# Attention and experts on one core: the second norm's transposes and the router logits in a fourth stage, a new table of places, and a reordered start

## The reference

```python
x = x + _layernorm(attn(_layernorm(x)))         # 16 heads of 8, causal, relative positions clipped to +-2
x = x + _layernorm(ffn(_layernorm(x)))

# attn: Q, K, V = x @ W + b per head
scores = (Q K^T + Q . rel_k[idx]) / sqrt(8);  causal mask;  softmax
out    = (attn V + attn . rel_v[idx]) @ W_o + b_o
# ffn
shared = (silu(x @ sw1) * (x @ sw3)) @ sw2
s      = sigmoid(x @ router_w.T);  top 2 of s + router_bias;  gates = s_sel / sum
routed = sum over the two experts e of gate_e * (gelu(x @ ew1[e]) @ ew2[e])
```

## Time and profile before

| | us |
|---|---|
| median of 3 runs (1090.37 to 1091.61) | 1090.96 |
| the profiled execution | 1092.7 |
| its span, first to last instruction | 1090.6 |
| start, to the first score matmul | 48.7 |
| steps 1 to 17 | 724.2 (48.7 to 772.9) |
| rest of the first phase | 32.3 (to 805.2) |
| second phase | 285.4 |

### The profile page before, as it was taken

How to read it: one execution, slowest core, us unless ns; L and a number is a source line. 1 busy time by engine, 2 the same in 40 slices (tenths; PEclk the granted TensorE clock), 3 DMA queues, 4 the chain that set the end, 5 groups by cost and what they waited for, 6 DMA issues and landing times. The chain is left out here.

```text
span 1090.6 us, 25410 instructions
## 1 busy us (share of the span) xinstructions
PE 945.4 (87%) x8551; PEld 557.6 (51%) x8551; DVE 854.2 (78%) x2060; ACT 693.6 (64%) x1309; POOL 725.9 (67%) x935
## 2 busy tenths in 40 slices
PE   0378999999999999999999999996658999999995
PEld 0144455455454454554554544542246777777774
DVE  4187888888888888888888888887158888888884
ACT  3424776776776767767766768665235766676763
POOL 2133666768658668677586686665355988988986
PEclk9988999999999999999999999998669999999999
DMA  5100101101001001010010010102313545455551
GB/s 141 56 23 27 35 22 36 38 20 44 31 21 50 21 32 42 20 41 33 20 49 21 32 46 20 38 12 54 115 48 118 160 149 163 154 164 156 158 156 31
DMA packets 61452, 70.87 MB, mean 65 GB/s; under 512 B 9504, under 2 KB 39072, under 8 KB 61344
## 3 DMA queue, kind: packets, MB, share of 16 engines
q1 hardware_dynamic: 61344, 69.47, 20.4%
HBM read 43.75 MB, written 8.65 MB: 48 GB/s over the span
## 5 line engine op out<-in xcount | busy, mean ns | idle before, releaser
L1071 DVE TENSOR_REDUCE mx<-ps_s 128x1 f32<-128x512 f32 (+2 forms) x640 | 412.1, 683 | 94.6 <-PE ps_s L1458 89.9
L759 ACT ACTIVATE prob<-ps_e 128x512 f32<-128x512 f32 x640 | 348.6, 601 | 131.0 <-PE ps_e L1424 131.0
L614 POOL TENSOR_SCALAR_AFFINE_SELECT prob<-prob 128x516 f32<-128x516 f32 (+1 forms) x320 | 172.8, 564 | 187.4 <-ACT prob L759 187.4
L1447 PE MATMUL ps_s<-ks,qs 63*128 63x512 f16 (+3 forms) x1024 | 230.3, 308 | 36.8 <-DMA ks<-kl 17.0
L713 POOL TENSOR_TENSOR hidden_low<-hidden,hidden_high 128x512 fp32r<-128x512 f32 x144 | 190.4, 1350 | 21.5 <-ACT hidden_high L949 20.2
L1424 PE MATMUL ps_e<-qs,ks 64*128 64x512 f16 (+3 forms) x1024 | 185.3, 303 | 9.1 <-DMA qs<-mT 4.4
L1475 PE MATMUL ps_av<-prob,vp 128*32 128x512 f32 (+3 forms) x2048 | 181.5, 450 | 9.3 <-POOL prob L614 9.3
L1458 PE MATMUL ps_s<-maskb,identb 64*128 64x129 bf16 (+1 forms) x1024 | 142.7, 223 | 0.0
L1458 PE MATMUL ps_s<-maskr,identr 64*128 64x129 bf16 (+1 forms) x1024 | 140.3, 219 | 0.0
L1447 PEld LDWEIGHTS ps_s<-ks,qs 63*128 63x128 f16 x1024 | 81.0, 94 | 100.0 <-DVE mx L1071 71.6
L949 ACT CAST hidden_high<-hidden 128x512 fp32r<-128x512 f32 x160 | 98.1, 613 | 34.6 <-DVE hidden L1372 30.4
(11 more groups left out here) (176 smaller groups left out, 1802.9 us busy)
## 6 DMA issues: line engine op xcount, KB each, us to landing
gate_rows<-gates_dram SPq DMA_DIRECT2D x128, 256.0 KB, 3.5
qs<-qh SPq DMA_DIRECT2D x128, 32.0 KB
qs<-ql SPq DMA_DIRECT2D x128, 32.0 KB
ks<-kh SPq DMA_DIRECT2D x128, 32.0 KB
ks<-kl SPq DMA_DIRECT2D x128, 32.0 KB
xnT_dram<-oT SPq DMA_DIRECT2D x16, 256.0 KB, 2.0
xeT<-xnT_dram SPq DMA_DIRECT2D x16, 256.0 KB, 2.7
out<-result SPq DMA_DIRECT2D x16, 256.0 KB, 2.3
```

The costliest lines, as they stand in the source:

```text
L614: pool.affine_select(out=v, in_=v, compare_op=ALU.is_ge, fill=0.0, base=-2, pattern=cols, channel_multiplier=-1).then_inc(S["p_masked"], 1)
L759: act.activation(prob[g % 2][:, u, b, :], ps_e[bank][:, :], ACT.Exp, scale=SCALE).then_inc(S["e_done"], 1)
L1071: dve.tensor_reduce(out, src, AX.X, ALU.max).then_inc(s_free[bank], 1)
L1447: pe.matmul(scores[:, at:at + P * (qt + 1)], qs[par][rows, 2 * g + off, P * qt:P * qt + P], ks[par][rows, 2 * g + off, 0:P * (qt + 1)], st ...
```

## The change

- A fourth stage D, on sequence t-4, takes xn2 (norm and transposes) and logits out of C; there are 20 steps. GpSimd's second norm stands in the next step, behind two masks. xn2's transposes go to round 5 and the logits to round 9.
- The places are chosen anew: v0 and m1 earlier, xT from round 6 to 7, oT from 8 to 11, oproj and av0 from 10 to 12, on the engines that read them too; the first AV part of each group from round 1 to round 2 of its five.
- All of the gate work of step 17 stands in one piece.
- SP's store of xn2T stands behind the maxima of the other half, and before step 18's gate stores.
- Start: VectorE begins with step 0's statistics, and all constants stand behind them. The loads are split: eleven for q and k on SP (`qk_loaded`), eight on ScalarE's queue (`attn_loaded`). TensorE needs the output bias only in step 2. The key rows are filled by one copy of VectorE per buffer instead of a memset and two copies of ScalarE. The first eight transfers of ks come from ScalarE, beside SP's eight of qs. The load of x for sequences 2 to 15 stands behind SP's eight.
- Checks of counts per step go away with no instruction.

```diff
-AT = {"e_sums": 1, "av2": 2, "v1": 3, "v0": 5, "m1": 5, "av3": 6, "xT": 6, "s_tok": 7, "oT": 8, "q": 9,
-      "av0": 10, "oproj": 10, "k": 10, "m0": 15, "av1": 17, "xn2": 18, "logits": 19}
+AT = {"e_sums": 1, "av2": 2, "m1": 3, "v1": 3, "v0": 4, "xn2": 5, "av3": 6, "s_tok": 7, "xT": 7, "q": 9,
+      "logits": 9, "k": 10, "oT": 11, "av0": 12, "oproj": 12, "m0": 15, "av1": 17}
 STAGE = {"av2": "C", "e_sums": "A", "m1": "B", "s_tok": "A", "av3": "C", "v0": "A", "v1": "A", "oT": "C", "xT": "F",
-         "oproj": "C", "q": "F", "k": "F", "av0": "B", "m0": "A", "av1": "B", "xn2": "C", "logits": "C"}
+         "oproj": "C", "q": "F", "k": "F", "av0": "B", "m0": "A", "av1": "B", "xn2": "D", "logits": "D"}
...
 def steps(eng, body):
-    for t in range(NSEQ + 3):
+    for t in range(NSEQ + 4):
...
         @block.sync
         def _(sp):
             def load(dst, src):
-                sp.dma_start(dst, src, allow_slow_non_contiguous=True).then_inc(S["attn_loaded"], 16)
+                sp.dma_start(dst, src, allow_slow_non_contiguous=True).then_inc(S["qk_loaded"], 16)
 
             sp.dma_start(xr[:, 0, :].rearrange("p (i d) -> p i d", i=NT), x_v[:, 0]).then_inc(x_loaded[0], 16)
-            for dst, src in ((wq_in, W_q), (wk_in, W_k), (wv, W_v), (wo, W_o)):
+            for dst, src in ((wq_in, W_q), (wk_in, W_k)):
                 load(dst[:, :], src)
-            load(rwT[:, :], router_w.rearrange("e d -> d e"))
+            load(rk_all[:, :, :], rel_k[0:3, :].partition_broadcast(P))
             for dst, src in ((bq, b_q), (bk_in, b_k)):
                 for c in range(4):
                     load(dst[32 * c:32 * c + 32, :], split_heads(src)[c // 2, c % 2])
-            load(rk_all[:, :, :], rel_k[0:3, :].partition_broadcast(P))
-            load(bv_col[:, :], b_v.rearrange("(d o) -> d o", o=1))
-            load(rv0_col[:, :], rel_v[0, :].partition_broadcast(H))
-            load(bo_in[:, :], b_o.partition_broadcast(P))
-            load(rv[:, :, :], rel_v[0:3, :].partition_broadcast(P))
-            load(rb[:, :], router_bias.partition_broadcast(P))
 
             sp.dma_start(xr[:, 1, :].rearrange("p (i d) -> p i d", i=NT), x_v[:, 1]).then_inc(x_loaded[1], 16)
...
+                    if s == 0 and half == 0 and stk is ks[par]:
+                        continue
...
-                masks(0, 1)
                 if st.B:
                     near_half(st, st.b, 1)
-                masks(1, 2)
+                masks(0, 2)
+                if st.D:
+                    normalise(st, st.d, xn2[:, :, :], tiles(xr[:, st.d, :]), mv3, var3, rs3,
+                              "stats3").then_inc(S["xn2_ready"], 1)
+                masks(2, 3)
                 if st.F:
                     normalise(st, st.f, xn[:, :, :], tiles(xr[:, st.seq(st.f), :]), mv1, var1, rs1,
                               "stats1").then_inc(S["xn_ready"], 1)
-                masks(2, 10)
+                masks(3, 6)
                 if st.F:
                     split(st)
...
                                        ALU.add).then_inc(S["x1_ready"], 1)
-                if st.t0 == 1:
-                    selectors()
-                masks(12, 15)
-                if st.C:
-                    normalise(st, st.c, xn2[:, :, :], tiles(xr[:, st.c, :]), mv3, var3, rs3,
-                              "stats3").then_inc(S["xn2_ready"], 1)
...
+            def load(dst, src):
+                act.dma_start(dst, src, allow_slow_non_contiguous=True).then_inc(S["attn_loaded"], 16)
+            load(wv[:, :], W_v)
+            load(wo[:, :], W_o)
+            load(rwT[:, :], router_w.rearrange("e d -> d e"))
+            load(bv_col[:, :], b_v.rearrange("(d o) -> d o", o=1))
+            load(rv0_col[:, :], rel_v[0, :].partition_broadcast(H))
+            load(bo_in[:, :], b_o.partition_broadcast(P))
+            load(rv[:, :, :], rel_v[0:3, :].partition_broadcast(P))
+            load(rb[:, :], router_bias.partition_broadcast(P))
+            def first_keys():
+                act.wait_ge(S["k_rows"], 1)
+                act.wait_ge(S["qk_split"], 2)
                 for b in range(2):
+                    for r, part in enumerate((kh, kl, kh, kl)):
+                        lo = HALF * b + D * r
+                        act.dma_start(ks0[lo:lo + D, 0:NPAIR // 2, :],
+                                      part[HALF * b:HALF * b + 32, :]).then_inc(stacks[0][0], 16)
...
-                exps(1, 2)
+                exps(1, 4)
                 if st.B:
                     p_near_exp(st, st.b, 1)
-                exps(2, 9)
+                    mT_out(st, st.b, 1)
+                exps(4, 7)
...
+                exps(7, 9)
+                if st.D:
+                    xn2T_out(st)
+                exps(9, 14)
...
+                exps(20, 21)
+                if st.D:
+                    logits_out(st)
+                exps(21, 22)
+                if st.C:
+                    oT_out(st)
+                exps(22, 23)
...
-                exps(34, 35)
-                if st.C:
-                    xn2T_out(st)
...
+            def key_buffers(i):
+                dve.wait_ge(S["const_ready"], N_POOL_CONST)
+                dve.tensor_copy(ks[i][:, :, :].bitcast(F32).rearrange("p n c -> p (n c)"), m_col[:, :].bitcast(
+                    F32).to_broadcast([P, NPAIR * SEQ // 2])).then_inc(S["k_rows"], 1)
...
-                maxima(15, 20)
+                maxima(14, 22)
+                if st.A:
+                    max_half(st, st.a, 0)
+                maxima(22, 24)
+                if st.B:
+                    av_tok_out(st, st.b, 0)
                 if st.C:
                     y_out(st)
-                if st.A:
-                    max_half(st, st.a, 0)
-                maxima(20, 21)
+                    y_bn(st)
+                maxima(24, 25)
                 if st.C:
-                    y_bn(st)
                     aggregate(st2, mv2, "stats2")
-                maxima(21, 24)
+                maxima(25, 30)
+                if st.t0 == NSEQ + 1:
+                    dve.wait_ge(S["misc_free"], Step(NSEQ + 1).misc("logits") + 1)
+                    gates_scores(0, EARLY)
+                    gates_second(0, EARLY)
+                    gates_shares(0, EARLY)
+                maxima(30, 34)
                 if st.B:
-                    av_tok_out(st, st.b, 0)
-                maxima(24, 25)
-                if st.t0 == NSEQ + 1:
-                    gates_shares(0, EARLY)
-                if st.t0 == 0:
-                    buffers(1)
-                maxima(25, 31)
+                    av_tok_out(st, st.b, 1)
+                maxima(34, 36)
                 if st.C:
                     x1_bn(st)
+                maxima(36, 37)
+                if st.C:
                     aggregate(st3, mv3, "stats3")
-                maxima(31, 36)
-                if st.B:
-                    av_tok_out(st, st.b, 1)
-                maxima(36, 40)
-                own.end()
+                maxima(37, 40)
+                if st.t0 == 0:
+                    key_buffers(0)
+                    qk_constants()
+                    value_buffers(0)
+                    other_constants()
+                    key_buffers(1)
+                    value_buffers(1)
+                    bias_out()
...
+                if st.t0 == 1:
+                    pe.wait_ge(S["const_ready"], N_CONST)
+                    pe.wait_ge(S["rolled"], 4)
+                    pe.matmul(ps_av[:, 0:P], bias_v[:, :], wo[:, :], start=True, stop=True).then_inc(S["bias_full"], 1)
+                if st.t0 == 2:
+                    pe.wait_ge(S["bias_ready"], 1)
+                here = {"F": st.F, "A": st.A, "B": st.B, "C": st.C, "D": st.D}
...
-                    for kt in {1: (0,), 2: (1, 2,), 3: (3,)}.get(u, ()):
+                    for kt in {2: (0, 1, 2,), 3: (3,)}.get(u, ()):
...
-            pe.wait_ge(S["const_ready"], N_CONST)
-            pe.wait_ge(S["rolled"], 4)
-            pe.matmul(ps_av[:, 0:P], bias_v[:, :], wo[:, :], start=True, stop=True).then_inc(S["bias_full"], 1)
-            pe.wait_ge(S["bias_ready"], 1)
+            pe.wait_ge(S["const_ready"], N_POOL_CONST)
```

215 lines of the change are left out of this document (94 added, 121 removed).

## The result

The changed kernel takes **1113.6 us** (median of 4 runs, 1112.0 to 1115.3) against 1091.2 for the kernel before on the same chip: ratio 1.021, 95% interval 1.019 to 1.023. It is slower by 22.4 us; the forecast was 1058.3 us, 32.7 faster. The change as a whole lost 22 us although its start gained 18.

The account below looks back on a forecast made before the run. TensorE was busy 491.0 of 518.9 us in twelve steps, leaving start, steps and drain: -19.2 - 12.9 - 2.6 + 2.0 = -32.7, giving 1058.3 us; own range 1050 to 1067, eight in ten 1042 to 1076.

Parts of the forecast that it names:

- Start, -19.2: Kernel start: reordered constants, loads and two queues bring the first score matmul from 48.7 to 29.5 us.
- The second queue: Start: ScalarE issues the eight ks transfers beside SP's eight of qs, 8 x 0.70 = 5.6 us less.
- The 4 us between are the cover: Step 1: x load lands by 45, second-half stacks behind it are needed at about 49, so no wait.
- I count nothing for it: AV block, steps: eight matmuls of each group move a round later; TensorE's work stays the same, priced at nothing.
- rival (4): AV blocks meeting empty banks: eight moved matmuls cost 1.0 us four times a step, 1114 us; chance 0.04.
- What is late next is GpSimd's chain: Head of step: xn2 arrives 0.4 to 0.8 us ahead, xT 0.3 to 0.7 late; miss up to 1 us possible.
- All work stays: Steps, fourth stage: four transposes (0.6 us) and eight logit matmuls (1.0 us) per sequence remain.
- The 0.8 us at xn2: Steps 3 to 16: TensorE's wait for GpSimd's second norm goes, 14 x 0.8 = 11.3 us.
- the bound of -2.4 a step: Steps: m0's row chain lets a step shrink by no more than 2.4 us unless shortened.
- Drain, -2.6 + 2.0: Step 17's gates end at 39.6 us instead of 42.2 (-2.6); step 18 gets sequence 14's xn2 and logits (+2.0).

Follow-up runs that it names:

- start_only: Kernel before with only the new start, its old places kept and no fourth stage: 1074.3 us, ratio 0.988.
- start_av: start_only with the changed kernel's AV blocks (24 matmuls in the third round of five, 8 in the fourth): 1115.2 us.
- idle_av: stage_idle with the changed kernel's AV blocks (24 and 8 matmuls), nothing else: 1095.9 us.
- near_xn: Changed kernel with kd(1), near products and near_half at their old places and GpSimd's two norms exchanged: 1166.3 us.
- changed_mended: pool_mended with the old AV blocks (8, 16, 8 matmuls) and VectorE's max_half behind maximum 20: 1179.5 us.
- stage_norm: start_only plus the fourth stage, GpSimd's second norm behind mask 4 of the next step: 1100.2 us.
- max_apart: Changed kernel with VectorE's max_half of the first half behind maximum 20 instead of 22: 1101.7 us.
- stage_idle: stage_norm with GpSimd's second norm behind mask 5 instead of 4, xn2's transposes and av0 one round later: 1049.5 us.
- pool_mended: Changed kernel with GpSimd's norms, q and k split, near products and near_half in stage_idle's order, AV blocks as changed: 1082.8 us.

## Why the prediction was wrong

- **Start, -19.2: near, in part by luck.** -18.3 by the traces, -15.8 in start_only by the medians (1090.1 to 1074.3). The product started at 12.3, 2.0 earlier than forecast; the time from there to the first matmul was 17.9 instead of 15.2, and the two errors nearly cancel. Of the 2.7 too much, 2.2 lie between the last issue and the matmul (3.85 instead of 1.7), which half of the traces don't have. The second queue was worth 4.7 by the traces (5.8 by medians of different groups) for the 5.6 said; the issue, not the transfer, was what was long, as the rows had shown. "The 4 us between are the cover" was wrong: the stacks came late at step 1's score unit 20, by 2.6 us in the changed kernel and 1.8 in start_only.
- **"I count nothing for it" (the AV block): the step that failed most.** It was priced as rival (4), 1.0 us four times a step, and given 0.04. By itself it costs 2.9 to 3.0 a step (start_av, idle_av). The mechanism was the rival's, though smaller than the 4.0 of its price: about 2 at the full clock in start_av, and 0.9 that the fallen clock adds; 2.9 at nearly full clock (mean 0.99) in idle_av. The argument against it, that TensorE waits for VectorE's banks, so that they are full more often than empty, took a mean for a place: the waits before a block and the idle time behind it stand in the same rows.
- **The near chain: not in the sum at all.** Moving kd(1) by three exponentials and the products by three masks was passed over as part of "the places are chosen anew", with 1.0 us a step behind it. The first norm's statistics on VectorE, moved by four maxima, have no term either; they cost nothing that shows in the changed kernel, but hold up masks in near_xn and changed_mended.
- **"What is late next is GpSimd's chain": right place, wrong victim.** The forecast asked what arrives late for xn2 and xT, and xT does wait, 0.4 us a step (bound: 1 us). But it never asked which masks stand behind the two norms, and which AV part waits for them. In stage_norm that is 2.3 us, in near_xn 3.2. In the changed kernel the late AV blocks hide it (0.2 us a step for masks), at their own price.
- **"All work stays": wrong.** The instructions stay, but VectorE's time for them grew by 3.1 us a step; in the rows it is small operations, most with two SBUF inputs, that now run beside GpSimd. With 1.9 of it gone (max_apart), 11.8 us came back.
- **The 0.8 us at xn2: went, as forecast.** And the bound of -2.4 a step held: stage_idle reaches -1.8 (43.26 to 41.49).
- **Drain, -2.6 + 2.0: mis-sized.** It was +6.6. y was put at 18 us behind the step's start and came at 27.2 (773.18 less 746.0), behind the read of av0, and the gates ended at 46.9 instead of 39.6, past even the bound of 45.6. In stage_idle, where oproj stayed at round 10, they ended at 40.1.
- **The parts don't add up.** In start_only's surroundings the AV blocks cost 41, the near chain 16 and the stage 26, 83 in all; together, with the rest of the table, they cost 39 (1113.6 less 1074.3). Late AV blocks hide late masks. So a share of the loss can't be given to each part, only what taking it out or putting it in does in a named surrounding.

The range of 1042 to 1076 would have held stage_idle and start_only, kernels with one or two of the ideas of the change. The change itself had more edits in it: the AV blocks and the near chain, put into start_only alone, cost 41 and 16 us, where the new start had gained 15.8.

## What to carry to other kernels

On engines that work in order, price a moved instruction by what stands behind it in that engine's queue, and who waits for that; the moved norm was worth -25 or +26 us by one mask's position. When two engines both run near their limit and hand each other three banks, a block that fills none for longer than the banks last costs time, however full the banks are on average: here 2.1 us against three banks of 0.65 cost 0.5 to 0.7 us a block, more than the 0.2 that the lengths differ by. Small operations with two SBUF inputs belong where GpSimd is idle, and a table of places should be changed one line at a time.

## What the runs showed of the hardware

The clock added to some of the stalls. In one step of the changed kernel TensorE was busy for 1.2 of 2.4 us, at the wait for the bank of oT, and then ran at the lower level of 1.2 GHz for about 3 us (busy by stretch):

```profile
366.20:367.40 1.20, 0.66 (x4) 0.42 (x4) 1.17 (x4) 1.17 (x3) 0.64 (x1) 1.00 0.00 0
367.40:368.60 1.20, 0.55 (x7) 0.27 (x8) 1.17 (x2) 1.20 (x4) 1.20 (x2) 1.00 0.00 0
368.60:369.80 1.20, 1.20 (x16) 1.03 (x13) 1.13 (x3) 1.20 (x4) 1.20 (x3) 0.71 0.03 7
369.80:371.00 1.20, 1.20 (x7) 1.20 (x7) 1.20 (x3) 0.53 (x2) 1.20 (x4) 0.50 0.08 27
```

The step from 340.9 us has two such stretches and takes 46.1 instead of 45.3 us; one with one takes 45.7. With one stretch it is 46.9 instead of 45.2 in start_av, and 44.2 instead of 42.8 in pool_mended. It doesn't follow each time: the same wait stands in each of the seven steps, and the clock fell in two of them; from 320.3 to 322.7 us TensorE was busy for 1.05 of 2.4 us and kept the full clock. stage_idle, with TensorE busy for 97%, has no such stretch in eight steps. So a stall in the middle of a busy phase can be dearer than its own length.
